# A linear-attention chain on one core: the three products of a chunk in one PSUM bank, its output in another, and a new table of steps

## What is computed

```python
q = silu(conv4(x @ Wq)); k = silu(conv4(x @ Wk)) * DK**-0.5; v = silu(conv4(x @ Wv))
alpha = sigmoid(x @ Wa + ba); beta = sigmoid(x @ Wb + bb)
def step(S, (qt, kt, vt, at, bt)):            # one token
    err = S kt - vt
    S = at * S - bt * (err outer kt)
    return S, S qt
o = layernorm(outputs) * ln_w + ln_b
out = (o * sigmoid(x @ Wg)) @ Wo
```

## Time and profile before

| | |
|---|---|
| median of 3 runs | 3739.14 us (3737.49 to 3743.43) |
| the profiled execution's own time | 3737.92 us |
| its span, first to last instruction | 3736.3 us |
| busy share of the span: PE, DVE, ACT, POOL | 96%, 63%, 62%, 52% |
| visits 0 of the turns, first to last (the attention part at full load) | 521 to 3295 us |
| matmuls with the output projection | 3378 to 3729 us |

### The profile page before, as it was taken

The page is one execution under the profiler, slowest core; times in us unless marked ns, Lnnn a source line. Parts: engine busy times, 40 slices in busy tenths (PEclk is TensorE's granted clock), DMA queues, the critical chain, the costliest instruction groups (busy, mean ns, idle before and its releaser), DMA issues. The chain is left out here.

```text
span 3736.3 us, 106429 instructions
## 1 busy us (share of the span) xinstructions
PE 3570.4 (96%) x32416; PEld 2924.9 (78%) x32416; DVE 2344.3 (63%) x5756; ACT 2298.5 (62%) x6401; POOL 1956.5 (52%) x4898
## 2 busy tenths in 40 slices
PE   7999969999999999999999999999999999978999
PEld 5777757888888888888888888888888888856887
DVE  4444446777777777777777777777777777743222
ACT  3434437777777777777777777777777777742111
POOL 3344535666666666665666666666666666630000
PEclk9999989999999999999999999999999999978999
DMA  4343342332333333333533333333333333316443
GB/s 151 116 147 113 125 131 67 81 76 75 75 82 77 73 79 89 77 73 79 134 110 74 82 75 76 78 79 76 73 80 89 76 73 81 73 30 188 143 143 112
DMA packets 420118, 348.65 MB, mean 93 GB/s; under 512 B 190448, under 2 KB 323568, under 8 KB 415728
## 3 DMA queue, kind: packets, MB, share of 16 engines
q1 hardware_dynamic: 417008, 333.60, 33.7%
q0 software_dynamic: 2560, 8.39, 0.6%
...
## 5 line engine op out<-in xcount | busy, mean ns | idle before, releaser
L1131 DVE SCALAR_TENSOR_TENSOR conv<-bank,tap,conv 128x512 f32<-128x512 f32 x1152 | 861.6, 748 | 143.7 <-ACT conv L1268 123.5
L1330 PE MATMUL bank<-hx_hi,w_hi 128*128 128x512 f32 x1536 | 667.6, 435 | 0.0
L1330 PE MATMUL bank<-hx_hi,w_lo 128*128 128x512 f32 x1536 | 632.5, 412 | 20.3 <-DVE Tnb L1093 19.1
L1330 PE MATMUL bank<-hx_lo,w_hi 128*128 128x512 f32 x1536 | 648.8, 422 | 0.0
L970 POOL TENSOR_TENSOR prods<-Lb,Tc 128x60 f32<-128x60 f32 (+14 forms) x1920 | 482.5, 251 | 277.1 <-DMA Lb<-base_d 134.0
L977 POOL TENSOR_TENSOR Tc<-Tc,prods 128x56 f32<-128x56 f32 (+13 forms) x1792 | 461.7, 258 | 142.0 <-POOL prods L970 3.1
L1249 ACT ACTIVATE Wc<-bank 128x128 f32<-128x128 f32 x512 | 142.3, 278 | 380.8 <-PE bank L1416 351.4
L1085 DVE SCALAR_TENSOR_TENSOR S<-S,gamma,bank 128x128 f32<-128x128 f32 x480 | 163.2, 340 | 337.0 <-PE bank L1427 336.9
L1012 POOL TENSOR_TENSOR oG<-oT,gT 128x512 f32<-128x512 f32 x128 | 164.9, 1288 | 388.8 <-ACT oT L1289 388.8
L1330 PEld LDWEIGHTS bank<-hx_hi,w_lo 128*128 128x128 f32 x1536 | 293.0, 191 | 61.6 <-DVE Tnb L1093 23.9
L1330 PEld LDWEIGHTS bank<-hx_hi,w_hi 128*128 128x128 f32 x1536 | 292.2, 190 | 41.5
...
## 6 DMA issues: line engine op xcount, KB each, us to landing
Lb<-base_d SPq DMA_DIRECT2D x128, 512.0 KB, 4.6
gamma<-gamma_d SPq DMA_DIRECT2D x128, 258.0 KB, 4.3
alpha<-alpha_d SPq DMA_DIRECT2D x128, 256.0 KB, 3.2
oT_d<-oG SPq DMA_DIRECT2D x128, 256.0 KB
...
```

The costliest lines, as they stand in the source:

```text
L1131: dve.scalar_tensor_tensor(out=conv[i][:, to], in0=PJ[PJ_OF[g][i]][:], scalar=tap[:, i, j + 1:j + 2], in1=conv[i][:, to], op0=ALU.mult, op ...
L1330: last = pe.matmul(dst, a[:, i, k], b[:, k], start=(j == 0), stop=(j == 3 * KC - 1))
```

## The change

The constants of the table get new values, and the chain is rearranged:

- CO is one bank. Its quarters hold kT S, TT R and k_rows Wc of every chunk. The output has a bank OB of its own, the same one for all chunks.
- q_gamma S moves from link r = 2 to link r = 1, right behind TT R. It now waits that the output of the chunk before was copied out of OB (`o_copied`).
- In link r = 2, k_rows Wc comes first and AT Wc second. The first raises `chain_done`, the second a new semaphore `out_done`, for which the copies of the output, AT's rewrite and the clearing of S wait.
- kT S does not wait for `o_copied` any more.

The core of the diff (of the table the lines that the rows below don't show in full):

```diff
-CHAIN = {1: 0, 6: 1, 8: 2, 11: 3, 15: 4, 18: 5, 19: 6, 22: 7, 23: 8, 26: 9, 30: 10, 36: 11}
+CHAIN = {0: 0, 7: 1, 8: 2, 11: 3, 15: 4, 18: 5, 19: 6, 22: 7, 23: 8, 26: 9, 28: 10, 36: 11}
-MT32_AT, TT64_AT, MT64_AT, TT128_AT = 21, 4, 27, 6
+MT32_AT, TT64_AT, MT64_AT, TT128_AT = 26, 12, 35, 4
-O_AT = {16: 0, 28: 1, 29: 2, 1: 3}
+O_AT = {13: 0, 17: 1, 25: 2, 1: 3}
-CUT_AT = {(3, 20): 0, (3, 23): 1, (3, 36): 2, (0, 18): 3}
+CUT_AT = {(3, 13): 0, (3, 21): 1, (3, 28): 2, (0, 19): 3}
...
-        PJ, WL, WH, TR, CO = bank[0:3], bank[3], bank[4], bank[5], bank[6:8]
+        PJ, WL, WH, TR, CO, OB = bank[0:3], bank[3], bank[4], bank[5], bank[6], bank[7][:, 0:D]
...
-                        act.wait_ge(s_done, at(4, -back, c + 2))
+                        act.wait_ge(out_done, at(4, -back, c + 1))
...
                     if r == 0 and not first:
                         pe.wait_ge(s_done, at(4, 0, c + 1))
-                        wait(pe, o_copied, at(4, 0, c - 1))
-                        pe.matmul(w[:, 0:D], kT[:, n % 6, chunk(c)], S[:], start=True, stop=True)\
-                          .then_inc(chain_done, 1)
+                        pe.matmul(CO[:, 0:D], kT[:, n % 6, chunk(c)], S[:], start=True, stop=True).then_inc(chain_done, 1)
...
                             pe.wait_ge(r_done, at(4, 0, c + 1))
-                            pe.matmul(w[:, D:2 * D], TT[:, n % 3, c], R[:], start=True, stop=True).then_inc(chain_done, 1)
+                            pe.matmul(CO[:, D:2 * D], TT[:, n % 3, c], R[:], start=True, stop=True)\
+                              .then_inc(chain_done, 2 if final else 1)
+                            if c == 0:
+                                pe.wait_ge(q_gamma_done, at(1, 1))
+                            wait(pe, o_copied, at(4, 0, c))
+                            pe.matmul(OB[:], q_gamma[:, cur, chunk(c)], S[:], start=True, stop=False)
                     if r == 2:
                         pe.wait_ge(w_done, at(4, 0, c + 1))
+                        if not final:
+                            if c == 0:
+                                pe.wait_ge(k_done, at(1, 1))
+                            pe.matmul(CO[:, 2 * D:3 * D], k_rows[:, cur, c], Wc[:], start=True, stop=True)\
+                              .then_inc(chain_done, 1)
                         if c == 0:
-                            pe.wait_ge(k_done, at(1, 1))
                             pe.wait_ge(at_done, at(1, 1))
-                            pe.wait_ge(q_gamma_done, at(1, 1))
-                        if not first:
-                            pe.matmul(w[:, 3 * D:], q_gamma[:, cur, chunk(c)], S[:], start=True, stop=False)
-                        last = pe.matmul(w[:, 3 * D:], AT[:, cur, c], Wc[:], start=first, stop=True)
-                        if not final:
-                            last = pe.matmul(w[:, 2 * D:3 * D], k_rows[:, cur, c], Wc[:], start=True, stop=True)
-                        last.then_inc(chain_done, 1)
+                        if first:
+                            wait(pe, o_copied, at(4, 0, c))
+                        pe.matmul(OB[:], AT[:, cur, c], Wc[:], start=first, stop=True).then_inc(out_done, 1)
```

More of the change, by code:

```diff
@@ L56 @@
             [(1, 1), (1, 2), (1, 3), (0, 0)], [(1, 1), (1, 2), (1, 3), (0, 1)]]
-A_AT, KT_AT, VT_AT, ON_TURN_AT, L_AT = 5, 2, 8, 22, 18
+A_AT, KT_AT, VT_AT, ON_TURN_AT, L_AT = 4, 1, 9, 22, 18
 VISIT_AT = {20: 0, 1: 1}
-SOLVE_AT = {37: (0, 1), 0: (1, 4), 1: (4, 6), 4: (6, 9), 7: (9, 11), 9: (11, 14), 11: (14, 15)}
-T16P_AT, POW_AT, QG_AT, OG_AT, DIAG_AT, LC_AT = 11, 15, 28, 29, 18, 17
-AT_AT, K_AT, T16_AT, TN64_AT, DECAY_AT, LT_AT = 6, 4, 18, 16, 7, 18
-BN_AT, AGGR_AT, ON_AT = 4, 5, 19
-YB_AT, TT_AT = 35, 0
-CONV_AT = {8: (0, 0), 9: (0, 1), 12: (0, 2), 19: (1, 0), 22: (1, 1), 23: (1, 2), 32: (2, 0), 33: (2, 1), 35: (2, 2)}
-VSILU_AT, GATE_AT, DIAGB_AT, VROWS_AT, KSILU_AT, QSILU_AT, OT_AT = 1, 16, 0, 14, 15, 30, 29
-PLACE_AT = {30: (0, 1), 7: (2, 3)}
-TN_PLACE_AT = 6
-MT32_AT, TT64_AT, MT64_AT, TT128_AT = 21, 4, 27, 6
-O_AT = {16: 0, 28: 1, 29: 2, 1: 3}
-TAP_AT = {14: 0, 17: 1, 28: 2}
-CUT_AT = {(3, 20): 0, (3, 23): 1, (3, 36): 2, (0, 18): 3}
+SOLVE_AT = {34: (0, 1), 0: (1, 4), 3: (4, 6), 4: (6, 9), 7: (9, 11), 10: (11, 14), 12: (14, 15)}
+T16P_AT, POW_AT, QG_AT, OG_AT, DIAG_AT, LC_AT = 12, 13, 24, 25, 22, 18
+AT_AT, K_AT, T16_AT, TN64_AT, DECAY_AT, LT_AT = 7, 4, 18, 17, 7, 18
+BN_AT, AGGR_AT, ON_AT = 4, 6, 20
+YB_AT, TT_AT = 31, 3
+CONV_AT = {8: (0, 0), 10: (0, 1), 14: (0, 2), 21: (1, 0), 22: (1, 1), 25: (1, 2), 26: (2, 0), 33: (2, 1), 34: (2, 2)}
+VSILU_AT, GATE_AT, DIAGB_AT, VROWS_AT, KSILU_AT, QSILU_AT, OT_AT = 1, 23, 3, 10, 15, 35, 24
+PLACE_AT = {32: (0, 1), 6: (2, 3)}
+TN_PLACE_AT = 4
+MT32_AT, TT64_AT, MT64_AT, TT128_AT = 26, 12, 35, 4
+O_AT = {13: 0, 17: 1, 25: 2, 1: 3}
+TAP_AT = {7: 0, 17: 1, 26: 2}
+CUT_AT = {(3, 13): 0, (3, 21): 1, (3, 28): 2, (0, 19): 3}
 SOLVE_PER = 2 * (SB - 1)
@@ L691, in heads @@
         chain_done = sem("chain_done")
+        out_done = sem("out_done")
         k_turned = sem("k_turned")
@@ L1042, in turn @@
                         dve.wait_ge(decay_done, at(1, 2))
-                        wait(dve, chain_done, at(12, 0))
+                        wait(dve, out_done, at(4, 0))
                         dve.tensor_tensor(AT[:, par], WL[:].rearrange("p (c t) -> p c t", c=G),
@@ L1074, in turn @@
                                 dve.wait_ge(scale_loaded[cur], row_loads(hh, g))
-                            dve.scalar_tensor_tensor(out=R[:], in0=CO[c % 2][:, 0:D], scalar=scale[:, cur, c:c + 1],
+                            dve.scalar_tensor_tensor(out=R[:], in0=CO[:, 0:D], scalar=scale[:, cur, c:c + 1],
                                                      in1=v_rows[:, cur, c], op0=ALU.mult, op1=ALU.add)\
@@ L1078, in turn @@
                         if r == 2:
-                            dve.wait_ge(chain_done, at(12, 0, k + 1))
+                            if g == 3 and c == 3:
+                                dve.wait_ge(out_done, at(4, 0, 4))
+                            else:
+                                dve.wait_ge(chain_done, at(12, 0, k + 1))
                             dve.wait_ge(s_done, at(4, 0, c + 1))
@@ L1085, in turn @@
                                 dve.scalar_tensor_tensor(out=S[:], in0=S[:], scalar=gamma[:, cur, c, C:C + 1],
-                                                         in1=CO[c % 2][:, 2 * D:3 * D], op0=ALU.mult, op1=ALU.add)\
+                                                         in1=CO[:, 2 * D:3 * D], op0=ALU.mult, op1=ALU.add)\
                                    .then_inc(s_done, 1)
@@ L1247, in turn @@
                         act.wait_ge(chain_done, at(12, 0, k + 1))
-                        act.activation(Wc[:], CO[k // 3 % 2][:, D:2 * D], ACT.Copy, scale=S_K).then_inc(w_done, 1)
+                        act.activation(Wc[:], CO[:, D:2 * D], ACT.Copy, scale=S_K).then_inc(w_done, 1)
                     if s in O_AT and (chain if O_AT[s] < 3 else ln):
                         c, back = O_AT[s], 1 if O_AT[s] == 3 else 0
-                        act.wait_ge(s_done, at(4, -back, c + 2))
+                        act.wait_ge(out_done, at(4, -back, c + 1))
                         if c == 0:
                             wait(act, on_done, at(4, -1))
-                        act.activation(o[:, (g - back) % 2, c], CO[c % 2][:, 3 * D:], ACT.Copy).then_inc(o_copied, 1)
+                        act.activation(o[:, (g - back) % 2, c], OB[:], ACT.Copy).then_inc(o_copied, 1)
                     if proj and s in TAP_AT:
@@ L1395, in chain_step @@
                     c, r = divmod(k, 3)
-                    w = CO[c % 2]
                     first, final = g == 0 and c == 0, g == 3 and c == 3
@@ L1410, in chain_step @@
                             pe.wait_ge(v_done, at(1, 1))
-                            wait(pe, o_copied, at(4, 0, c - 1))
-                            pe.matmul(w[:, D:2 * D], TT[:, n % 3, c], v_rows[:, cur, c], start=True, stop=True)\
+                            pe.matmul(CO[:, D:2 * D], TT[:, n % 3, c], v_rows[:, cur, c], start=True, stop=True)\
                               .then_inc(chain_done, 2)
```

## The result

| | before | after |
|---|---|---|
| median of 4 runs | 3740.47 us (3737.49 to 3743.43) | 3696.35 us (3695.74 to 3697.90) |
| ratio, 95% interval | | 0.988 (0.9868 to 0.9892) |
| span of the profiled execution | 3736.3 us | 3696.3 us |
| busy share PE, DVE, ACT, POOL | 96, 63, 62, 52% | 96, 65, 63, 53% |

The forecast was 3678 us, with a range from 3640 to 3735. The sign was right, and 44 us of the 62 came.

What follows compares the result with a forecast made beforehand. PE was taken to bound the kernel: 83.1 + 0.92 + 0.90 + 0.5 + 0.23 = 85.65 us per head against 87.51. Over 31 heads, 31 x 1.95 = 60 us less gave 3678 us, range 3640 to 3735.

Steps and rivals of the forecast that it cites:

- A head of PE work without a stall: PE's time per head with all waits taken off: 87.0 - 3.9 = 83.1 us, unchanged by the change.
- Step 6 (now 7): First TT v of a head, waiting for ACT's copies of TT: 0.72 us goes, perhaps 0.1 left.
- Steps 23 and 36: Third and fourth chunk's output, late for Wc: 0.54, 0.75 and 0.20, then 0.70 us per head, all to go.
- Steps 7 and 8: TT R to k_rows Wc: new stall of 0.17 us in three groups, 0.39 in group 0, together 0.90.
- step 28: kT S to TT R: 0.69 us of cover against 0.82, new stall 0.23 in all four groups, 0.92.
- A late product: On PE, its pair takes 0.32 us instead of 0.22; the skill's rule would give 0.8 us per head less, near 3653.
- The output bank: q_gamma S waiting for ACT's output copy: taken as zero, bound 1 us per turn; as slower rival, chance 0.10, 3753 to 3803.
- I keep 0.5 per head: PE's waits at visit 0 for the solve loop's Tnb: 0.5 us per head, bounds 0 and 1.6.
- I take nothing: Store of oG issued right behind the read of Lb queues behind it: zero, bound 0.5 us per turn.
- the stalls that PE loses at steps 6, 20, 23 and 36: PE's old waits for TT, Tnb and Wc: 0.72, 0.74, 0.54 + 0.75 + 0.20 and 0.70 us per head.
- the solve loop takes over: Rival, chance 0.17: visit 0 waits stay at 0.74 us in group 0, 0.3 elsewhere; head 86.8, time 3715.

Runs made afterwards that it cites:

- the run with the store back: Changed kernel with the output's turning and gating back in step 29, so oG's store issues some 3 us behind the read of Lb: 3682.24 us.
- the inversion short: Changed kernel with the last of the inversion's 15 steps left out, so part of the inverse isn't computed: 3668.72 us.
- the last experiment on the split: Changed kernel with TT R back in steps 6 and 30 and output turning and gating in 29 (3661.15 us), group 3's first weight split moved from step 13 to 20: 3673.98 us.

## Why the prediction came out as it did

**What held.** A head of PE work without a stall measures 86.43 - 3.44 = 82.99 us, by the steps' mean lengths less their undisturbed ones; 83.1 was the estimate. Step 6 (now 7) keeps 0.11 us, as said. Steps 23 and 36 have no stall left. Steps 7 and 8 cost 0.94 us a head (0.90 predicted), step 28 1.02 (0.92). A late product costs 0.33 us for its pair, as the earlier trace rows had it; by the rule that weight loads run ahead of matmuls in flight, which the Trainium skill (TensorE: Matmul & The Clock Gate, Part 2) states, the time would have been 3653, and the trace of after doesn't bear that out for a product whose operand comes late. The output bank costs nothing in this table.

**What failed.** The head was to be 85.65 us and is 86.43, 0.8 us or 24 us over 31 heads. The total is off by less, since the stretch behind the last visit 0 came out 6 us shorter; the sum had no term for that, and it is luck. A slip went the other way: 87.51 less 85.65 is 1.86 us, not the 1.95 that I multiplied by 31, so the sum really gives 3681 us. The terms:

- "I keep 0.5 per head": the visit waits measure 1.00. I took the loop's length from one turn, 20.8 us from LT to Tnb, and set it beside PE's 20.8. From LT to the end of Tnb the means are 21.2 to 21.7 us in groups 0 to 2 of the kernel before, and 22.8 in group 3, as the table of the loop's parts gives them. The turn I read was shorter than any of the means. With the means I would have seen that the loop, not PE, sets the pace in about half of the turns, above all across the boundary of groups 3 and 0, and that 0.5 was the lower end.
- "I take nothing" for the store behind the read of Lb, with a bound of 0.5 us per turn: 0.15 to 0.39 us in the three turns where the store came near, and 14 to 17 us in all, by the run with the store back. This is no term beside the first: with the store back the visit waits are 0.71 us, step 22 of group 3 loses 0.24, and the head is 0.45 us shorter, more than half of the 0.8 that were missing. I had seen the new distance and had the price at the lower bound, though the operation on which the loop turns was at the end of that transfer.
- Step 22 of group 3 takes 1.57 us instead of 1.27: the turning of the normed output waits there. I had no term for it. It goes when the store is back (1.31) or the inversion short (1.28), so it hangs on the loop, and the last experiment on the split shows that taking it away alone brings nothing.

**Right for the wrong reason.** The sum put the gain down to the stalls that PE loses at steps 6, 20, 23 and 36, and mentioned the split only as the reason of one visit's delay. The runs say otherwise. Taking 1.9 us per head of PE stalls out of the changed kernel brings 10 us instead of 59. Putting one split back into the inversion takes 41 of the 44 us. So the gain needed two things at once: PE's stalls gone, so that PE is not longer than the loop, and the split out of the loop of group 3, so that the loop is not longer than PE. One of them alone is worth little: the split's move alone 8 us, everything but the split's move 4 us, or some 13 by an estimate that puts down to the low clock what the 41 us have over the split's own 1.04 x 31 = 32 us. Taking the stall at step 23 away alone proves nothing here, since it came back at step 26. The rival "the solve loop takes over" was the nearer description; its price (3715) was too high because I had not given the loop itself a gain of 1.1 us in group 3.

What stays open is why the stretch behind the last visit 0 takes 428 to 445 us from kernel to kernel, and why the clock falls behind some waits of PE and not behind others of the same length.
